# All four key blocks of the product with V in one place of TensorE's order, and ScalarE's copy of the output moved behind it

## The reference

```python
x = x + attn(cond(x, cond_1024, weight), w_qkv, w_out)
x = x + ffn(cond2(x, cond_1024, W_router, bias, s_w1, s_w3, s_w2, r_w1, r_w2), W1, b1, W2, b2, Wa, Wb)
```

```python
scores = jnp.einsum('bhsd,bhtd->bhst', q, k) / scale
scores = jnp.where(causal[None, None], scores, -jnp.inf)
attn = jax.nn.softmax(scores.astype(jnp.float32), axis=-1)
out = jnp.einsum('bhst,bhtd->bhsd', attn, v)
```

## Time and profile before

| | |
|---|---|
| device time, median of 3 runs | 183.96 us (181.8 to 184.19) |
| the profiled execution: span from first to last instruction | 180.1 us |
| its own whole time | not listed; the median is 3.9 us above the span |
| TensorE busy | 169.0 us (94%), 934 matmuls |
| VectorE busy | 139.3 us (77%) |
| ScalarE busy | 134.4 us (75%) |
| GpSimd busy | 93.4 us (52%) |
| product with V, matmuls (line 1466) | 256 instructions, 20.6 us |
| exps of the attention (line 1105) | 48 instructions, 40.8 us |
| maximum reductions (line 772) | 128 instructions, 58.8 us |

### The profile page before, as it was taken

The page is one execution under the profiler, slowest core; times in us unless marked ns, Lnnn a source line. Parts: engine busy times, 40 slices in busy tenths (PEclk is TensorE's granted clock), DMA queues, the critical chain, the costliest instruction groups (busy, mean ns, idle before and its releaser), DMA issues.

```text
span 180.1 us, 3258 instructions
## 1 busy us (share of the span) xinstructions
PE 169.0 (94%) x934; PEld 116.8 (65%) x934; DVE 139.3 (77%) x444; ACT 134.4 (75%) x224; POOL 93.4 (52%) x116
## 2 busy tenths in 40 slices
PE   6998989999999999988999999996999989999992
PEld 2765555765666666654648767874677867788881
DVE  5598899789898989981586998699889648637551
ACT  3569366687787788889735696953969999999970
POOL 4508188975453969696541632021769931676000
PEclk9999999999999999999999999999999999999999
DMA  4824673776666756421110799970760000001001
GB/s 132 305 46 103 179 208 118 231 257 233 177 203 187 198 181 184 157 78 49 58 55 9 217 294 361 338 229 11 234 233 0 0 4 0 0 2 58 0 4 58
DMA packets 15349, 24.28 MB, mean 135 GB/s; under 512 B 2844, under 2 KB 4828, under 8 KB 15308
## 3 DMA queue, kind: packets, MB, share of 16 engines
q1 hardware_dynamic: 14532, 23.29, 42.0%
q10 hardware_dynamic: 800, 0.79, 1.7%
HBM read 18.71 MB, written 5.27 MB: 133 GB/s over the span
## 4 chain that ended last, share of the span: by engine, by line
PE 70%; DVE 14%; ACT 8%; issue 5%; POOL 1%; ACTq 0%; DVEq 0%; POOLq 0%
PE psum L1405 11%; PE psum L1538 10%; PE psum L1466 9%; PE psum L1539 9%; PE psum L1540 9%; PE psum L1441 7%; DVE psum L772 4%; PE psum L1341 2%; PE psum L1355 2%; PE psum L1287 2%; ACT t_probs L1105 2%; PE psum L1445 2%; DVE t_raw L924 1%; PE psum L1400 1%; ACT t_q_pad L1155 1%
## 5 line engine op out<-in xcount | busy, mean ns | idle before, releaser
L772 DVE CUSTOM_DVE_ANT_0 psum<-psum,t_causal 128x128 f32<-128x128 f32 (+3 forms) x128 | 58.8, 525 | 6.0 <-PE psum L1405 3.3
L1105 ACT ACTIVATE t_probs<-psum 128x1024 f32<-128x1024 f32 (+2 forms) x48 | 40.8, 883 | 8.4 <-PE psum L1441 5.5
L1405 PE MATMUL psum<-t_stacked,t_q_pad 96*128 96x256 f32 (+2 forms) x104 | 32.1, 378 | 2.4 <-DVE t_row_max L772 1.2
L1405 PEld LDWEIGHTS psum<-t_stacked,t_q_pad 96*128 96x128 f32 x104 | 17.7, 188 | 16.3 <-DVE t_row_max L772 11.2
L672 POOL TENSOR_SCALAR_AFFINE_SELECT t_probs<-t_probs 128x512 f32<-128x512 f32 x32 | 20.5, 653 | 9.0 <-ACT t_probs L1105 8.3
L944 DVE SCALAR_TENSOR_TENSOR t_q_pad<-psum,t_zw_all,t_q_pad 128x512 fp32r<-128x512 f32 x24 | 17.8, 748 | 9.4 <-ACT t_q_pad L1153 9.3
L1139 ACT ACTIVATE psum<-psum 128x512 f32<-128x512 f32 x40 | 23.4, 586 | 1.2 <-PE psum L1540 0.6
L703 POOL TENSOR_TENSOR t_q_pad<-t_raw,t_q_pad 128x512 fp32r<-128x512 f32 x8 | 10.8, 1358 | 21.0 <-ACT t_q_pad L1155 21.0
L1466 PE MATMUL psum<-t_probs,t_v_all 128*32 128x512 f32 (+3 forms) x256 | 20.6, 439 | 0.0
L772 DVE DVE_READ_ACCUMULATOR2_ANT t_row_max<- 128x1 f32 x128 | 18.2, 142 | 0.0
L1153 ACT ACTIVATE t_q_pad<-psum,t_zw_all 128x512 fp32r<-128x512 f32 x24 | 16.5, 689 | 1.2 <-PE psum L1540 0.5
(11 more groups left out here) (232 smaller groups left out, 366.2 us busy)
## 6 DMA issues: line engine op xcount, KB each, us to landing
t_stacked<-scratch SPq DMA_DIRECT2D x16, 256.0 KB, 5.7
t_probs<-in_L_ffn_Wa SPq DMA_DIRECT2D x2, 1024.0 KB, 13.1
scratch<-t_o_sb SPq DMA_DIRECT2D x7, 256.0 KB, 2.0
t_raw<-in_experts SPq DMA_DIRECT2D x7, 256.0 KB, 3.1
t_stacked<-scratch SPq DMA_DIRECT2D x9, 192.0 KB, 2.7
t_q_pad<-scratch SPq DMA_DIRECT2D x28, 48.0 KB
scratch<-t_dn_hi SPq DMA_DIRECT2D x2, 512.0 KB, 3.2
t_q_two<-scratch SPq DMA_DIRECT2D x5, 192.0 KB, 2.6
```

The source lines that it names most:

```text
L772: last = V.tensor_tensor_reduce(scores, scores, causal[:, S - width:S], 1.0, 3 * BIG, ALU.add, ALU.max, row_max[s][:, qb, j:j + 1])
L1105: A.activation(o, scores, ACT.Exp, scale=float(1.0 / np.sqrt(np.float32(HD)))).then_inc(exp_done, 1)
L1405: last = T.matmul(bank[:, o:o + width], q_pad[s][0:TOP, j, qb * P:(qb + 1) * P], stacked[0:TOP, n, 0:width], start=True, stop=True)
```

## The change

In TensorE's order, `weigh_v` of all four key blocks of group n - 1 stands in period n behind exp scores 2. Key blocks 1 to 3 stood ahead of the fourth slice of maximum units in that period, and key block 0 behind exp scores 4 in the group's own period. After the last period all four key blocks of group 7 stand behind `up(0)`, where three stood. On ScalarE the copy of the output of group n - 1 stands behind exp 3 of period n instead of behind exp 1. No instruction is added or removed, and no wait is changed.

```diff
@@ scalar engine, attention loop
                 exp(n, 1)
-                if 0 < n < GROUPS - 1:
-                    copy_pv(n - 1)
                 exp(n, 2)
                 if (n, 0) in SPLITS:
                     split_high(SPLITS[n, 0])
                 exp(n, 3)
+                if 0 < n < GROUPS - 1:
+                    copy_pv(n - 1)
                 exp(n, 4)
@@ tensor engine, attention loop
                 maximum(1)
                 maximum(2)
-                if n:
-                    weigh_v(n - 1, 1, P, S)
-                    weigh_v(n - 1, 2, 2 * P, S)
-                    weigh_v(n - 1, 3, 3 * P, S)
                 maximum(3)
                 scores_for_exp(n, 2)
+                if n:
+                    for kb in range(KB):
+                        weigh_v(n - 1, kb, kb * P, S)
                 if n == GROUPS - 1:
                     project_out(0)
                 scores_for_exp(n, 3)
...
                 scores_for_exp(n, 4)
                 if n == GROUPS - 1:
                     route_experts(0)
-                weigh_v(n, 0, 0, S)
                 maximum(7)
...
             up(0)
-            weigh_v(GROUPS - 1, 1, P, S)
-            weigh_v(GROUPS - 1, 2, 2 * P, S)
-            weigh_v(GROUPS - 1, 3, 3 * P, S)
+            for kb in range(KB):
+                weigh_v(GROUPS - 1, kb, kb * P, S)
```

## The result

The changed kernel takes 190.44 us (median of 4 runs, 188.11 to 191.69); the kernel before took 182.93 in the 4 runs beside it (181.8 to 184.19). The ratio is 1.037, 95% interval 1.029 to 1.046. The forecast was 190.4.

The account below looks back on a forecast made before the run. TensorE and VectorE, coupled by a three-bank ring, bound the kernel together. Start -0.35, steady periods +4.0, end +2.7 and SyncE +0.1 sum to +6.4 us: span 186.5, plus 3.9 carried, 190.4 us; range 186 to 193.5.

Parts of the forecast that it names:

- Half of it: Steady period: TensorE as only bound is half the story; VectorE, fed through a three-bank ring, is within 0.8 us.
- T to u0: From the first 512-wide maximum unit's reduction end to the next group's first reduction start: 4.04 us, VectorE dry about 1.8.
- u0 to T: From the group's first 256-wide reduction start to its first 512-wide reduction end: 4.97 us, TensorE keeping ahead.
- SyncE: Later output stores delay padded q and k loads in the one iteration with the gather: 0.1 us, bounds 0 and 1.
- ScalarE: Steady period: waits for exp scores 3 behind the block, busy 7.5 of 9.0 us, so doesn't set the period.
- Period 0: Key block leaves the first period, but the laying of the maxima is late next: -0.35 us (0 to -1.0).
- The end: Last two periods, to the up unit behind block 7: +2.7 us, 1.0 to 3.2; exp 0 of group 7 +1.1.
- The expert and zone stages ... give nothing back: Stages after attention, bound by TensorE and VectorE in turn, run as before: 0 us.
- The clock at 1.0 throughout: Whole execution: TensorE's granted clock was to stay at 1.0.
- The first: Rival: TensorE alone is the bound and half the block edges go: -2.2 us, 181.8; chance 0.13.
- The second: Rival: VectorE starves as forecast, but the last two periods lose only 0.5: +3.7 us, 187.6; chance 0.15.
- The third: Rival: q and k loads come late in every period, up to 1 us each: +4 on the forecast, 194; chance 0.10.

Follow-up runs that it names:

- The later gather: Changed kernel with SyncE's gather issued behind group 7's padded q and k, and the reciprocal of its sums two units later: 190.19 us, ratio 1.040.
- the kernel whose clock never fell: Changed kernel with twelve unread matmuls filling TensorE's gaps in periods 6 and 7: 189.18 us, ratio 1.037.
- the two pads: Changed kernel with extra TensorE work in periods 1 to 5: exp scores 5 computed three times, 189.66 us; separately, exp scores 3 computed twice, 192.11 us.
- the new end alone: Groups 0 to 4 in the order of the kernel before, groups 5 to 7 in the changed order: 185.74 us, ratio 1.011.
- the swapped u10: Kernel before with the four-head maximum unit moved one place earlier, ahead of the block of three key blocks: 181.38 us, ratio 0.995.

## Why the prediction was right, and where its sizes were off

**The bound.** "Half of it": confirmed. TensorE's 0.43 us cost nothing in one stretch and 0.35 us cost 0.35 in the other, in the same kernel. Before, 0.33 of the 0.43 showed, so there the two engines were nearly level, as read from the earlier trace rows.

**T to u0**: 4.04 forecast, 4.13 measured (57.04 to 61.17), VectorE dry 1.84 for 1.8. The block itself, 2.31 forecast, took 2.29 (57.88 to 60.17); what was 0.09 short is the way around it. **u0 to T**: 4.97 and 5.00. Together the period was 0.9 over 8.23, not 0.8: over five steps that is +4.48 for +4.0 without the queue.

**SyncE**: 0.1 forecast, in truth 0.43, all in the one period with the gather, as the mechanism said. Both sizes lay inside their bounds. The fifth period follows this wait in the experiments: 9.56 where it is 0.49, 9.58 with it at 0.16 under a longer block, and 9.56 with it at 1.20 where the other periods are 8.41. The later gather removed it, and opened another.

**ScalarE**: it waits 1.52 and sets nothing. The move of the copy alone costs 3.96 us on the old order, and leaving it out costs 0.7 on the new one: the two edits belong together.

**Period 0**: -0.35 and -0.36. The laying of the maxima was late next, as said.

**The end**: +2.7 forecast; +2.27 at full clock, both in the kernel whose clock never fell and in the profiled execution less the dip's 1.53. Most of the missing 0.43 is one term: exp 0 of group 7 was to come 1.1 later against T and came 0.75 later (7.42 behind T for 6.67). Exp scores 3 were ready a little sooner than said, and ScalarE's exp 3, copy and exp 4 took 2.2 us together, not 2.4.

**Wrong steps.** "The expert and zone stages ... give nothing back": they gave 0.77 back, since the gates no longer ran beside GpSimd's masks. "The clock at 1.0 throughout": it fell behind the emptier periods 6 and 7 in the profiled execution. At full clock the misses nearly cancel: +0.48 (the periods) and +0.33 (SyncE) against -0.43 (the end) and -0.77 (behind it). That the sum came within 0.4 us is luck, though the longer period, the queue's edge, the gain in period 0 and the longer end each came about as described. The median of 190.4 came out equal also because both kernels' medians hold runs with the early dip (the three runs of before that I started from had a median of 183.96, with two of them at 184); at full clock the forecast's size, +6.4, met 6.3. The range's arithmetic had a slip that nothing hung on: the lower bounds as listed add up to 187.5, not 186.5.

**Rivals.** The first (TensorE alone, 181.8) falls with the two pads. The second (the end loses little, 187.6): the new end alone is only +1.2 in its run at clock 1.0 (3.7 by the medians, where its runs hold one dip or both), but the stretch to the last up unit lost over 2.2 in every reading. The third (SyncE late in every period) showed in one of five.

## What to carry to other kernels

Where engines pass work through a ring, ask for each block in the producer's order how much work lies in the ring when it begins, in the consumer's microseconds: a block longer than that leaves the consumer dry for the excess and for the way to its next unit, here 1.84 us for 0.51 before, however busy the producer looks. A unit that can't be issued until the ring frees a bank is a bad thing to put ahead of a long block (0.41 us of the 0.90 a period); a unit that is cheap to make and long to consume is a good one, as the swapped u10 shows (0.7 us gained). And moving several small pieces into one saves only edges, here 0.13 us a pair (2.29 for 0.99 + 1.43), while it makes the longest interruption longer.

## What the runs showed of the hardware that was not expected

**The clock of an emptier stretch.** TensorE was busy 2.24 of 4.00 us, at clock 1.00, and in the 4 us behind it the clock was 0.65; the same block of 32 instructions took 3.50 us for 2.36. The profiles of all seven other kernels that have the four blocks together in the last periods show such a dip behind a window with 2.1 to 2.5 of 4.00 us busy, and so does the kernel before with the late copy alone (2.41 of 4.00, then 0.50). It doesn't come in every execution: at least one run each of four of these kernels, the changed one among them, is at clock 1.0. With the gaps filled none of six runs had it (three at clock 1.0, the others at the 0.98 of the early dip). An order that leaves gaps can pay for them twice. The early dip (0.50 from 20 to 24 us, 2.22 us) comes and goes with the same program, and nothing here explains it.

**Small VectorE operations behind GpSimd's masks.** A conversion of 8 elements took 0.53 us beside a mask and 0.17 without; a comparison of 32 took 0.57 and ended at 93.73, 0.04 behind the mask's end at 93.69. The maximum and index searches beside the changed kernel's masks kept their times (0.37 for the four, as before). With masks of 128 columns (0.29 us each) both were shorter and ended again 0.03 and 0.05 us behind a mask: the conversion at 92.91 behind 92.88, the comparison at 93.18 behind 93.13. A rule of the Trainium skill (SBUF — State Buffer, "SBUF: two separate sides") says that VectorE and GpSimd have a pair of ports in common, which a GpSimd instruction, or a VectorE one with two SBUF inputs or in a mode that uses both ports, takes for its whole length while the other is blocked. For the comparison, which has two inputs, the trace agrees, by the ends that coincide. The conversion has one input, and no run shows which mode it ran in.
